# The first layer's bias: added by VectorE after an indirect gather, or laid down by broadcast transfers with the gather accumulating onto it

## The reference

```python
h = x @ W                                     # x: 50000 x 96
msg = h[src] * (inv_sqrt_out[src] * inv_sqrt_in[dst])[:, None]
agg = segment_sum(msg, dst, num_segments=N)
x = layernorm(x + (agg + b))                  # x + b: the residual and the bias of the first layer
```

## Time and profile before

| | |
|---|---|
| median of the three timed runs | 3838.0 us |
| span of the profiled execution (its first to its last instruction) | 3835.1 us |
| TensorE / VectorE / ScalarE / GpSimd busy | 1899.1 / 2675.0 / 2083.6 / 2663.3 us |
| line 572: first and last start | 156.8 and 647.7 us |
| first gather of layer0 (line 822) | 655.54 us |

### The profile page before, as it was taken

How to read it: one execution, slowest core, us unless ns; L and a number is a source line. 1 busy time by engine, 2 the same in 40 slices (tenths; PEclk the granted TensorE clock), 3 DMA queues, 4 the chain that set the end, 5 groups by cost and what they waited for, 6 DMA issues and landing times. The chain is left out here.

```text
span 3835.1 us, 43642 instructions
## 1 busy us (share of the span) xinstructions
PE 1899.1 (50%) x9253; PEld 1495.8 (39%) x9253; DVE 2675.0 (70%) x10319; ACT 2083.6 (54%) x4590; POOL 2663.3 (69%) x2767
## 2 busy tenths in 40 slices
PE   5466610777886888766666637887820000000000
PEld 2133300676775777654444427777820000000000
DVE  8899975677774666648888868889844444544544
ACT  8688820676772222224444536777755555555555
POOL 0277777777774777757777747777647777777776
PEclk9799965788885666665555556677655555555555
DMA  0111187455554666645666645555522222222222
GB/s 7 32 40 40 40 241 232 138 153 165 161 156 139 207 209 208 208 160 182 198 199 205 203 140 177 196 195 189 179 78 81 77 78 81 77 77 81 80 74 60
DMA packets 355635, 521.96 MB, mean 136 GB/s; under 512 B 213243, under 2 KB 224804, under 8 KB 355370
## 3 DMA queue, kind: packets, MB, share of 16 engines
q1 hardware_dynamic: 260986, 363.50, 28.1%
q0 software_dynamic: 94384, 155.67, 15.8%
HBM read 227.76 MB, written 291.22 MB: 135 GB/s over the span
## 5 line engine op out<-in xcount | busy, mean ns | idle before, releaser
L1984 PE MATMUL l_psR<-l_diag,l_ones 128*128 128x128 f32 x2 | 0.8, 501 | 1000.4 <-DVE l_diag L1839 1000.4
L1749 POOL DMA_INDIRECT l_G<-t,src x392 | 377.8, 964 | 164.7 <-issue 119.1
L1133 POOL DMA_INDIRECT l1b_G<-t,src x392 | 389.8, 994 | 135.8 <-issue 117.5
L1450 POOL DMA_INDIRECT l_G<-t,src x392 | 380.0, 969 | 141.7 <-issue 117.7
L1133 POOL DMA_INDIRECT l1a_G<-t,src x392 | 378.9, 967 | 138.0 <-issue 118.3
L1764 POOL DMA_INDIRECT out<-O,nidx x393 | 385.2, 980 | 128.4 <-issue 118.8
L822 POOL DMA_INDIRECT l_G<-xs,src x392 | 370.5, 945 | 126.1 <-issue 113.4
L572 POOL DMA_INDIRECT O<-x_pad,nidx x393 | 372.3, 947 | 119.7 <-issue 119.7
L1984 PEld LDWEIGHTS l_psR<-l_diag,l_ones 128*128 128x128 f32 x2 | 0.5, 313 | 1000.5 <-DVE l_diag L1839 1000.5
L179 ACT ACTIVATE O<-O,l_shift,l_rstd 128x96 f32<-128x96 f32 x786 | 292.6, 460 | 27.1 <-DVE l_shift L173 27.1
L1309 PEld LDWEIGHTS l1b_psE<-l1b_we,l1b_edge 32*128 32x128 f32 x784 | 174.2, 323 | 198.5 <-DMA l1b_edge<-edge_k 141.6
(11 more groups left out here) (311 smaller groups left out, 6404.6 us busy)
## 6 DMA issues: line engine op xcount, KB each, us to landing
h<-l_G SPq DMA_DIRECT2D x96, 392.0 KB, 2.8
t<-l1b_t_out SPq DMA_DIRECT2D x48, 768.0 KB
h<-l_G SPq DMA_DIRECT2D x48, 768.0 KB, 3.5
xs<-en_y SPq DMA_DIRECT2D x49, 392.0 KB, 5.2
en_y<-x_pad SPq DMA_DIRECT2D x49, 384.0 KB, 4.9
t<-l_t_out SPq DMA_DIRECT2D x48, 392.0 KB, 4.5
l_H<-t SPq DMA_DIRECT2D x48, 392.0 KB, 3.1
t<-l_tr_out SPq DMA_DIRECT2D x48, 384.0 KB
```

The costliest lines, as they stand in the source:

```text
L1133: pool.indirect_dma_start(tile(c)[:, q, :], None, table, bass.IndirectOffsetOnAxis(k.src[:, at:at + 1], 0))\
L1450: pool.indirect_dma_start(tile(c)[:, q, :], None, table, bass.IndirectOffsetOnAxis(k.src[:, at:at + 1], 0))\
L1749: pool.indirect_dma_start(tile(c)[:, q, :], None, t4, bass.IndirectOffsetOnAxis(k.src[:, at:at + 1], 0))\
```

## The change

`k.O` is filled with the bias by seven broadcast transfers on SP's queue, each over 56 columns (the last over 57), and every placing transfer becomes an accumulating one: it adds the 128 rows of `x` to what is in `k.O`. POOL waits for the first part of the fill before its first transfer, and for one more part after each seven chunks. The last part is issued when counting is over, since it writes the working space of counting. The tile `b0r`, its load, its copy into PSUM and DVE's fifty additions are gone. POOL and DVE wait for all placing transfers at the end.

```diff
+    FILL = 7
-        b0r = sb("b0r", [128, D])
-        factor, b0p = psC[:, 0:K], psC[:, K:K + D]
+        factor = psC[:, 0:K]
+        filled = [sem(f"filled{g}") for g in range(HELD_BACK // FILL + 1)]
         def _(sp):
             sp.dma_start(ends[:, 1, :], starts[1:2, :].to_broadcast([128, 128])).then_inc(loaded, 16)
-            sp.dma_start(b0r[:, :], b0.to_broadcast([128, D])).then_inc(loaded, 16)
+
+            def fill(g):
+                first = g * FILL * Q
+                end = min(first + FILL * Q, K) if g < HELD_BACK // FILL else K + 1
+                sp.dma_start(k.O[:, first:end, :], b0.unsqueeze(1).to_broadcast([128, end - first, D]))\
+                  .then_inc(filled[g], 16)
             for c in range(YRING - 1):
                 load(c)
+            for g in range(HELD_BACK // FILL):
+                fill(g)
+            sp.wait_ge(s_tallied, NHOT)
+            sp.wait_ge(tallied, NHOT + 1)
+            fill(HELD_BACK // FILL)
             for c in range(NCH):
                 sp.wait_ge(scaled, c + 1)
...
         def _(pool):
-                if c == HELD_BACK:
-                    pool.wait_ge(s_tallied, NHOT)
-                    pool.wait_ge(tallied, NHOT + 1)
+                if c % FILL == 0 and c <= HELD_BACK:
+                    pool.wait_ge(filled[c // FILL], 16)
                 for q in range(tiles(c)):
                     at = c * Q + q
                     pool.indirect_dma_start(k.O[:, at, :], None, x,
-                                            bass.IndirectOffsetOnAxis(k.nidx[:, at:at + 1], 0))\
-                        .then_inc(placed[c % RING], 16)
+                                            bass.IndirectOffsetOnAxis(k.nidx[:, at:at + 1], 0),
+                                            compute_op=ALU.add).then_inc(placed[c % RING], 16)
+            for s in range(RING):
+                pool.wait_ge(placed[s], 16 * sum(tiles(c) for c in range(s, NCH + 1, RING)))
...
         def _(dve):
-            dve.tensor_copy(b0p, b0r[:, :])
...
-            for c in range(NCH + 1):
-                if c < NCH:
-                    u = c % YRING
-                    dve.wait_ge(x_in[u], 16 * (c // YRING + 1))
-                    dve.tensor_tensor(y[:, u, :, 0:D], y[:, u, :, 0:D],
-                                      factor[:, c * Q:(c + 1) * Q].unsqueeze(2).to_broadcast([128, Q, D]),
-                                      ALU.mult).then_inc(scaled, 1)
-                dve.wait_ge(placed[c % RING], 128 * (c // RING) + 16 * tiles(c))
-                dve.tensor_tensor(k.O[:, cols(c), :], k.O[:, cols(c), :],
-                                  b0p.unsqueeze(1).to_broadcast([128, tiles(c), D]), ALU.add)
+            for c in range(NCH):
+                u, n = c % YRING, tiles(c)
+                dve.wait_ge(x_in[u], 16 * (c // YRING + 1))
+                dve.tensor_tensor(y[:, u, 0:n, 0:D], y[:, u, 0:n, 0:D],
+                                  factor[:, cols(c)].unsqueeze(2).to_broadcast([128, n, D]),
+                                  ALU.mult).then_inc(scaled, 1)
+            for s in range(RING):
+                dve.wait_ge(placed[s], 16 * sum(tiles(c) for c in range(s, NCH + 1, RING)))
```

More of the change, by code:

```diff
@@ L584, in _ @@
             dve.tensor_scalar(s_from[:, :], lo[:, 0:K], -1.0, 0.5, ALU.mult, ALU.add).then_inc(keyed, 1)
-            dve.wait_ge(loaded, 64)
+            dve.wait_ge(loaded, 48)
             dve.wait_ge(consts, 2)
```

## The result

The changed kernel takes 4206.7 us in the median of four runs, the kernel before 3839.2 us in the same measurement. One of the four runs, of 4296.5 us, had a lower granted clock and is left out of the ratio; without it the range is 4198.1 to 4208.5 and the median 4205.0. The ratio is 1.094, with an interval from 1.092 to 1.096: some 367 us slower, where +34 was forecast. The profiled execution has a span of 4206.8 us, 371.7 more than before.

What follows compares the result with a forecast made beforehand. POOL's instruction stream was taken to bound the kernel nearly everywhere. First-fill wait +21, accumulation +13 and removed work -0.3 summed to +34 us on the profiled 3835.1, giving 3872 us as timed; 8-in-10 range 3852 to 4235.

Steps and rivals of the forecast that it cites:

- The wait for the first fill: Entry stage, POOL: the first placing waits for the fill's landing and starts at 178 instead of 156.85, +21 us.
- The accumulating transfer: Each of POOL's 393 placings takes 33 ns more, priced like an indirect store, +13 us.
- What bounds the kernel: POOL's instruction stream sets the time nearly everywhere, about 1.25 us a column; DVE's work is hidden.
- DVE's fifty additions: Entry stage: removing them is worth nothing except the last, behind the last landing, -0.3 us.
- Fills 1 to 5 are never waited for: Entry stage: each takes 12.7 us against the 70 us in which POOL works through a part.
- Rival 1: Placing instruction: a packet for each row adds 154 to 560 ns, total 3920 to 4080 us; chance 0.26.
- Rival 2: Placing instruction: its work doubles, reading from two places, +944 ns each, total 4230 us; chance 0.14.
- The seventh fill and the scaling chain: Entry stage: first store +6 us, dearer placings +24; last store at about 673, hidden behind POOL's end at 682.
- Rival 4: Entry stage: scaling ends last, at 695, if the placings' share triples; 3885 us, within the forecast's range of chance 0.42.

Runs made afterwards that it cites:

- fill_from_sbuf: The changed kernel with its fills read from a bias tile in SBUF instead of one row of HBM: 5200.4 us, ratio 0.972 to a kernel before of 5363.
- plain_placing: The changed kernel with its seven fills kept and the accumulation taken out of the placings: 5393.6 us, ratio 1.006 to a kernel before of 5363.
- sbuf_fill_again: The same kernel as fill_from_sbuf, run again: 5199.9 us, ratio 0.972, beside a kernel before of 5357.
- sbuf_fill_plain_placing: The changed kernel with fills from the SBUF bias tile and placings without accumulation: 5368.9 us, ratio 0.999.

## Why the prediction was wrong

The steps that failed are two prices. The wait for the first fill was put at +21 us and measured +104.5, since its price came from rows in which no single place in HBM is read over and over. The accumulating transfers were put at +13 us and measured +239, since their price came from a transfer that doesn't add. The scaling chain's cover fell with the fill's price, another +30.

**What bounds the kernel** held outside the stage: POOL's stream, and nothing behind the stage moved (3178 against 3180 us). DVE's fifty additions were worth nothing: without them and with neither loss the kernel takes 20.5 us more (3855.4 - 3834.9), which is the wait for the first fill. At the end of the stage POOL's stream was no longer what bounds it.

**The wait for the first fill** failed, in size and in its reason. It was put at +21 (bounds +17 and +27) by packets of 384 bytes at 28.4 ns, and a sentence said that reading from one place is in no row and may be worse, but this got no bound and no rival. It measured +104.5. With the same bytes from SBUF or from 128 rows of HBM the step comes out as forecast: first placing at 176.6 to 177.6 against 178, +20.5 us on the total. The prediction's estimate of 8.3 us by the Trainium skill ("DMA: Bandwidth & Descriptors", anatomy of one DMA) rests on a fit that the page gives for transfers issued by GpSimd; quick fills, issued by SP, hold its queue for 11.2 us each in the median (fill_from_sbuf).

**"Fills 1 to 5 are never waited for"** held by luck of the other error: 98 us for a fill against 56 x 1.856 = 104 for a part. With plain placings POOL waited for all of them.

**The accumulating transfer** was mis-sized: +13 was taken, +239 measured. The instruction takes 1556 ns, 609 more. The choice fell on the indirect store as the nearest row, which shares the operands' places but does not add. Rival 1's top, 560 ns, was nearly right in size, and its picture of one packet for each row is what POOL's queue shows (144 packets in place of 32, so seven more on each engine, as the rival had it), but not as the whole cause, since with 80 packets each a plain gather costs 953 ns and an accumulating placing 1443. Rival 2 had 944 ns more on the instruction and 4230 us: its total lies 23 us from the result by two errors that cancel, for it had the instruction at 1888 ns and the fill at 21 us. The range of 8 in 10, 3852 to 4235, holds the result only through this rival, by luck. The Trainium skill ("Collectives: The Full Stack", on why ReduceScatter is half of AllGather) has two read descriptors for one in a reducing transfer. The trace does not bear out a doubling of POOL's instruction (1556 against 947 ns is 1.64 times), nor one that goes by rows: 64 rows fewer save only 122 of 1565 ns.

**The seventh fill and the scaling chain** failed too. The chain was seen as hidden with 9 us of cover; it became the last to end, 30 us behind POOL. Rival 4 had this outcome but by dearer placings, at 13 us. The cause is SP's queue: six fills of 98 us stand ahead of the seventh, and it ahead of the first store.

## What to carry to other kernels

A price that no row shows and that counts 393 times must not be taken from the row that looks most alike: bound it on both sides, and don't put the forecast near the lower bound without a reason. A broadcast from one row of HBM to all partitions did no harm at 128 pieces (the bias load of the kernel before, for which DVE waited 0.8 us) and cost 99 us at 7168: load it once into SBUF and repeat it from there. Where two losses run beside each other, undo each alone and both together. Here plain placings alone give back 25 us (4205.0 - 4180.1), quick fills alone 110 (4205.0 - 4094.6) and both together 350, so either alone would have made its cause look small.

## What the runs showed of the hardware

- Sixteen DMA engines that read one 384-byte row of HBM over and over get 28.8 GB/s, one piece in 13.3 ns over all engines, at a busy share of 15% (changed kernel, 175 to 255 us); from SBUF, from distinct rows or from 128 rows the same transfer lands in 15 to 16 us. The mechanism in the memory wasn't measured.
- An accumulating indirect transfer costs POOL 519 to 609 ns more than a plain one, mostly a fixed price, and moves each row as its own packet: 144 packets for 128 rows of 384 bytes, where a plain one has 32. What POOL does in that time is open.
- While the slow fills ran beside them, placings landed 58.6 us after issue in the median, 2.4 us before, and both queues passed exactly 12530 packets in 180 us: the engines seem to take one packet of each in turn. This was read from the rows, not tested.
- On the chip that stretched the kernel, the counting ran at full speed beside accumulating placings and at a ninth of it beside plain ones (at half, 84.1 us of DVE, in plain_placing, where POOL stands still between them). PE, PEld, DVE, ACT, POOL busy from 300 to 480 us in sbuf_fill_again and in sbuf_fill_plain_placing:

```profile
300.00:480.00 180.00, 116.90 (x654) 60.00 (x654) 174.85 (x382) 151.36 (x274) 150.71 (x97) 1.00 0.27 27
```

```profile
300.00:480.00 180.00, 23.94 (x68) 8.27 (x68) 19.64 (x41) 15.11 (x26) 135.25 (x137) 0.51 0.18 37
```

The same kernel with plain placings had 174.87 us of DVE in this stretch on the undisturbed chip. So on the other chip the changed kernel's repaired form was faster than the kernel before (0.972), for a reason that no run shows; the lesson here is to compare only with a kernel before that was measured beside it.
